# Second attention of a two-layer transformer block: two buffers of turned long tiles, and the value products moved to other steps

## The reference

```python
kf = jnp.repeat(kf, g, axis=1)          # 8 key heads, 4 query heads on each, 64 wide
v = jnp.repeat(v, g, axis=1)
scores = jnp.einsum('bhqd,bhkd->bhqk', q, kf) / jnp.sqrt(jnp.asarray(HD, dt))
scores = jnp.where(causal, scores, jnp.finfo(dt).min)
attn = jax.nn.softmax(scores, axis=-1)
out = jnp.einsum('bhqk,bhkd->bhqd', attn, v)
```

## Time and profile before

| | |
|---|---|
| median of three runs | 2429.59 us |
| the profiled execution | 2425.01 us, of which 2422.9 us are the span |
| TensorE busy | 2127.0 us (88%) |
| VectorE busy | 1499.6 us (62%) |
| ScalarE busy | 891.2 us (37%) |
| GpSimd busy | 511.2 us (21%) |
| mean granted TensorE clock | 0.96 |

### The profile page before, as it was taken

One profiled execution on the slowest core, in us unless ns is written; L12 is line 12 of the kernel. 1 busy time (PEld: TensorE's weight loads), 2 busy tenths in 40 slices (PEclk: granted clock), 3 DMA queues, 4 the chain that ended last, 5 costly groups with the idle time before them and its releaser, 6 DMA issues. The chain is left out here.

```text
span 2422.9 us, 53839 instructions
## 1 busy us (share of the span) xinstructions
PE 2127.0 (88%) x22256; PEld 1484.4 (61%) x22256; DVE 1499.6 (62%) x2380; ACT 891.2 (37%) x1858; POOL 511.2 (21%) x419
## 2 busy tenths in 40 slices
PE   4899969999996999868888988888986788799997
PEld 3677747777775788724444444444444666687776
DVE  4544323333324455468999889988894786177776
ACT  3322123222222300035656556565563232134443
POOL 0110112122220145401111111111112455221111
PEclk9999989999998999979999999999998898899999
DMA  4121144000005633233443334333342866541100
GB/s 153 71 88 36 71 154 144 17 26 17 9 0 212 198 126 122 106 83 83 104 109 90 98 81 112 102 89 98 81 119 85 262 210 194 178 144 52 53 1 35
DMA packets 183984, 242.99 MB, mean 100 GB/s; under 512 B 37744, under 2 KB 110768, under 8 KB 181072
## 3 DMA queue, kind: packets, MB, share of 16 engines
q1 hardware_dynamic: 182896, 239.59, 32.1%
q10 hardware_dynamic: 864, 0.21, 0.0%
HBM read 156.82 MB, written 82.90 MB: 99 GB/s over the span
## 5 line engine op out<-in xcount | busy, mean ns | idle before, releaser
L1479 ACT ACTIVATE a_prob<-ps,a_nmax 128x256 f32<-128x256 f32 (+7 forms) x512 | 377.4, 739 | 349.1 <-DVE a_nmax L1507 212.2
L1592 PE MATMUL ps<-a_kt,a_q 64*128 64x512 f32 (+5 forms) x1536 | 378.0, 533 | 88.0 <-ACT a_prob L1479 64.7
L1507 DVE TENSOR_REDUCE a_nmax<-ps 128x1 f32<-128x1024 f32 (+3 forms) x256 | 256.3, 1001 | 74.1 <-PE ps L1592 72.7
L1524 DVE STREAM_TRANSPOSE a_pt_long<-a_prob 128x512 f32<-128x512 f32 (+3 forms) x512 | 278.3, 582 | 0.0
L1592 PEld LDWEIGHTS ps<-a_kt,a_q 64*128 64x128 f32 x1536 | 142.0, 191 | 186.4 <-ACT a_prob L1479 117.1
L1606 PE MATMUL ps<-a_pt_long,a_v 32*64 32x256 f32 (+3 forms) x7808 | 228.0, 344 | 1.8 <-DVE a_pt_long L1524 0.2
L1991 DVE SCALAR_TENSOR_TENSOR f_part<-ps,f_gu_scale,f_part 128x512 f32<-128x512 f32 x264 | 184.7, 745 | 65.0 <-PE ps L2039 51.7
L1606 PEld LDWEIGHTS ps<-a_pt_long,a_v 32*64 32x64 f32 x7808 | 153.6, 131 | 103.4 <-issue 75.6
L1559 POOL TENSOR_TENSOR a_o<-a_left 128x256 f32<-128x256 f32 x128 | 90.4, 729 | 594.9 <-ACT a_left L1489 594.9
L2039 PE MATMUL ps<-f_xt_hi,f_gu 128*128 128x512 f32 x352 | 142.3, 404 | 22.1 <-DMA f_wd_lo<-scratch_wd 12.6
L843 POOL TENSOR_TENSOR f_hT_lo<-f_h,f_hT_hi 128x512 fp32r<-128x512 f32 x64 | 82.0, 1293 | 325.0 <-ACT f_hT_hi L826 325.0
(11 more groups left out here) (225 smaller groups left out, 4518.5 us busy)
## 6 DMA issues: line engine op xcount, KB each, us to landing
a_q<-scratch_QT SPq DMA_DIRECT2D x512, 64.0 KB, 2.1
scratch_QT<-k_qo SPq DMA_DIRECT2D x64, 256.0 KB, 2.3
a_v<-scratch_V SPq DMA_DIRECT2D x64, 256.0 KB, 4.7
scratch_OT<-a_o SPq DMA_DIRECT2D x32, 512.0 KB, 3.3
o_of<-scratch_OT SPq DMA_DIRECT2D x32, 512.0 KB, 5.5
o_packed<-in_packed SPq DMA_DIRECT2D x11, 768.0 KB, 6.8
f_xt_hi<-scratch_xt SPq DMA_DIRECT2D x8, 1024.0 KB, 7.3
f_xt_lo<-scratch_xt SPq DMA_DIRECT2D x8, 1024.0 KB, 9.1
```

Of the source, the lines that this page charges most:

```text
L1479: last = nc.scalar.activation(prob[:, n % PRING, s].rearrange("p (a w) -> p a w", w=w), SC[n % 2][:, a, 0:w], ACT.Exp, bias=nmax[:, n % 4, ...
L1507: nc.vector.tensor_reduce(nmax[:, n % 4, 0:1], SC[n % 2][:, :, 0:width(0, t)], AX.XY, ALU.max, negate=True).then_inc(maxed, 1)
L1524: last = nc.vector.transpose(pt[hf][:, lo:hi, h, t - FIRST[hf], :], src.rearrange("p (j k) -> p j k", k=32))
L1592: last = pe.matmul(sc[:, a, 0:w], q[r, slot, heads[a * hf], :], kt[r, b, keys], start=not masked, stop=True, skip_group_check=True)
```

## The change

- The long turned tiles get two buffers, used by units in turn: `pt_long` for key blocks 0 to 23 and `pt_wide` for blocks 24 to 31, which only tiles 6 and 7 have.
- Every tile is turned whole, two steps after its scores. A long tile of over 24 blocks takes two instructions (768 columns, and 256 or 128), one of at most 24 blocks takes one (768 or 640 columns). FRONT, BACK and `half_valued` go.
- The short values are placed at r = 26 to 30 (steps 2 to 6 of the next unit) and come ahead of the long ones, which are placed at r = 33 to 46 (steps 9 to 22 of the next unit). The evictions, spreads, scalings and stores follow.
- `rden` gets two buffers. To make room, the ring of queries goes from 4 to 3 and the ring of probabilities from 8 to 4.

```diff
-QRING = 4
-PRING = 8
+QRING = 3
+PRING = 4
...
-LONG_VALUES = {18 + i: range(3 * i, 3 * i + 3) for i in range(10)}
-LONG_VALUES[28] = range(30, 32)
-SHORT_VALUES = {31 + i: range(2 * i, 2 * i + 2) for i in range(8)}
-LONG_LEFT = {28: (0, 1), 29: (2, 3)}
-SHORT_LEFT = {38: (0, 1), 39: (2, 3)}
-LONG_STORE, SHORT_STORE = 34, 44
-LATEST = 45
+MAIN = 24
+LATER = 2
+
+SHORT_VALUES = {26: range(0, 3), 27: range(3, 6), 28: range(6, 9), 29: range(9, 13), 30: range(13, 16)}
+LONG_VALUES = {33: range(0, 2), 34: range(2, 4), 35: range(4, 6), 36: range(6, 8), 37: range(8, 10),
+               38: range(10, 11), 39: range(11, 12), 40: range(12, 14), 41: range(14, 16), 42: range(16, 19),
+               43: range(19, 22), 44: range(22, 25), 45: range(25, 29), 46: range(29, 32)}
+SHORT_LEFT = {31: (0, 1), 32: (2, 3)}
+LONG_LEFT = {47: (0, 1), 48: (2, 3)}
+SHORT_SPREAD, LONG_SPREAD = 27, 40
+SHORT_SCALE, LONG_SCALE = 32, 48
+SHORT_STORE, LONG_STORE = 36, 52
+LATEST = 53
...
-        pt = [sb(f"pt_{s}", [P, BLOCKS[i], HQ, 4, 32]) for i, s in enumerate(("long", "short"))]
+        pt_long = sb("pt_long", [P, 2, MAIN, HQ, 4, 32])
+        pt_wide = sb("pt_wide", [P, 2, BLOCKS[0] - MAIN, HQ, 2, 32])
+        pt_short = sb("pt_short", [P, BLOCKS[1], HQ, 4, 32])
...
-        rden = sb("rden", [P, 16])
+        rden = sb("rden", [P, 2, 16])
...
-                    wait(sp, valued, 2 * u - 1)
+                    wait(sp, valued, 2 * u - 2)
...
-                        act.wait_ge(turned, last_turn(n - PRING))
+                        act.wait_ge(turned, n - PRING + 1)
...
-                def turn(n, part):
+                def turn(n):
                     unit, hf, t, heads = place(n)
-                    if n % USTEPS == 0 and part == FRONT:
-                        wait(dve, half_valued, unit)
-                    elif n % USTEPS in (0, LONG):
-                        wait(dve, valued, 2 * unit + hf - 1)
+                    if n % USTEPS == 0:
+                        wait(dve, valued, order(unit - 2, 0) + 1)
+                    elif n % USTEPS == LONG:
+                        wait(dve, valued, order(unit - 1, 1) + 1)
                     dve.wait_ge(exped, n + 1)
                     blocks = 4 * (t + 1)
...
+                        if hf:
+                            last = nc.vector.transpose(pt_short[:, 0:blocks, h, t, :], src)
+                        else:
+                            near = min(blocks, MAIN)
+                            last = nc.vector.transpose(pt_long[:, unit % 2, 0:near, h, t - 4, :], src[:, 0:near, :])
+                            if blocks > MAIN:
+                                last = nc.vector.transpose(pt_wide[:, unit % 2, 0:blocks - MAIN, h, t - 6, :],
+                                                           src[:, MAIN:blocks, :])
...
                 for n in range(NSTEPS + LATEST):
                     if n < NSTEPS:
                         maxima(n)
-                    for u, r in at_step(n, TURNS):
-                        for i, part in TURNS[r]:
-                            turn(u * USTEPS + i, part)
+                    if LATER <= n < NSTEPS + LATER:
+                        turn(n - LATER)
...
+                    for u, r in at_step(n, SHORT_VALUES):
+                        values(u, 1, SHORT_VALUES[r])
                     for u, r in at_step(n, LONG_VALUES):
                         values(u, 0, LONG_VALUES[r])
-                    for u, r in at_step(n, SHORT_VALUES):
-                        values(u, 1, SHORT_VALUES[r])
```

More of the change, by code:

```diff
@@ L1388, in attention1, with order, turned_part @@
         evicted, o_done, o_stored = sem("evicted"), sem("o_done"), sem("o_stored")
-        half_valued = sem("half_valued")
         def width(hf, t):
             return (t + 1) * P // 2 if hf == 0 else (t + 1) * P
-        turn_order = []
-        for n in range(NSTEPS + LATEST):
-            for u, r in at_step(n, TURNS):
[L1397 to L1401, removed]
+        def order(u, hf):
+            return 2 * u + (1 if hf == 0 else 0)
+        def turned_part(u, hf, j):
+            if hf:
+                return pt_short[:, j], 0
+            if j < MAIN:
+                return pt_long[:, u % 2, j], 4
+            return pt_wide[:, u % 2, j - MAIN], 6
         with nc.Block() as block:
@@ L1461, in _ @@
                     for u, r in at_step(n, (LONG_STORE, SHORT_STORE)):
[L1462 removed]
+                        store_o(u, int(r == SHORT_STORE))
                 sp.wait_ge(o_stored, 16 * 2 * NU)
@@ L1484, in evict @@
                 def evict(u, hf, banks):
-                    half = 2 * u + hf
-                    act.wait_ge(valued, half + 1)
-                    wait(act, o_done, 4 * half)
+                    act.wait_ge(valued, order(u, hf) + 1)
+                    wait(act, o_done, 4 * order(u, hf))
                     for i in banks:
@@ L1519, in turn @@
                     dve.wait_ge(exped, n + 1)
                     blocks = 4 * (t + 1)
-                    lo, hi = {FRONT: (0, MIDDLE), BACK: (MIDDLE, blocks), WHOLE: (0, blocks)}[part]
                     for i, h in enumerate(heads):
-                        src = prob[:, n % PRING, (i * blocks + lo) * 32:(i * blocks + hi) * 32]
-                        last = nc.vector.transpose(pt[hf][:, lo:hi, h, t - FIRST[hf], :],
-                                                   src.rearrange("p (j k) -> p j k", k=32))
+                        src = prob[:, n % PRING, i * blocks * 32:(i + 1) * blocks * 32]
@@ new lines, in turn @@
+                        src = src.rearrange("p (j k) -> p j k", k=32)
+                        if hf:
+                            last = nc.vector.transpose(pt_short[:, 0:blocks, h, t, :], src)
[5 more added lines that the diff above has]
+                                                           src[:, MAIN:blocks, :])
@@ L1526, in turn @@
                     last.then_inc(turned, 1)
                 def invert(u, hf):
-                    half = 2 * u + hf
                     dve.wait_ge(exped, u * USTEPS + (LONG, USTEPS)[hf])
-                    wait(dve, spread_out, half)
-                    nc.vector.reciprocal(rden[:], den[:, hf, :]).then_inc(inverted, 1)
+                    wait(dve, spread_out, order(u - 1, hf) + 1)
+                    nc.vector.reciprocal(rden[:, hf, :], den[:, hf, :]).then_inc(inverted, 1)
                 for n in range(NSTEPS + LATEST):
@@ L1536, in _ @@
                         maxima(n)
-                    for u, r in at_step(n, TURNS):
-                        for i, part in TURNS[r]:
-                            turn(u * USTEPS + i, part)
+                    if LATER <= n < NSTEPS + LATER:
+                        turn(n - LATER)
                     for u, r in at_step(n, (LONG + 2, USTEPS + 2)):
-                        invert(u, r == USTEPS + 2)
+                        invert(u, int(r == USTEPS + 2))
             @block.gpsimd
@@ L1545, in spread_half @@
                 def spread_half(u, hf):
-                    half = 2 * u + hf
-                    pool.wait_ge(inverted, half + 1)
-                    wait(pool, valued, half)
+                    pool.wait_ge(inverted, 2 * u + hf + 1)
+                    wait(pool, valued, order(u, hf))
                     nc.gpsimd.tensor_tensor(spread[:].rearrange("p h t q -> p (h t) q"),
-                                            rden[:].unsqueeze(2).broadcast_to([P, 16, 32]),
+                                            rden[:, hf, :].unsqueeze(2).broadcast_to([P, 16, 32]),
                                             diag[:].unsqueeze(1).broadcast_to([P, 16, 32]), ALU.mult
@@ L1554, in scale_half @@
                 def scale_half(u, hf):
-                    half = 2 * u + hf
-                    wait(pool, o_stored, 16 * half)
+                    wait(pool, o_stored, 16 * order(u, hf))
                     for i in range(4):
-                        pool.wait_ge(evicted, 4 * half + i + 1)
+                        pool.wait_ge(evicted, 4 * order(u, hf) + i + 1)
                         nc.gpsimd.tensor_tensor(o[:, :, :, i, :], left[:, i, 0], left[:, i, 1], ALU.mult
@@ L1563, in _ @@
                 for n in range(NSTEPS + LATEST):
[L1564 to L1567, removed]
+                    for u, r in at_step(n, (SHORT_SPREAD, LONG_SPREAD)):
+                        spread_half(u, int(r == SHORT_SPREAD))
+                    for u, r in at_step(n, (SHORT_SCALE, LONG_SCALE)):
+                        scale_half(u, int(r == SHORT_SCALE))
             @block.tensor
@@ L1598, in value_block @@
                     t0, b, k = FIRST[hf], unit % NB1, j // 4
+                    part, p0 = turned_part(unit, hf, j)
                     for c in range(2):
@@ L1606, in value_block, with denominators @@
                             last = pe.matmul(out[:, :, a - t0:4, :], v[rows, b, j, :],
-                                             pt[hf][rows, j, c::2, a - t0:4, :],
```

(9 more changed lines are left out.)

2 lines of the change are left out of this document (1 added, 1 removed).

## The result

The changed kernel takes 2416.53 us (median of five runs, 2413.06 to 2421.49) against 2430.55 us before (five runs). The ratio is 0.9945, with a 95% interval of 0.993 to 0.996: faster by 14 us (0.6%), where 55 were forecast. The profiled execution took 2421.49 us with a span of 2419.1. It is the slowest of the five, and its mean granted clock (0.950) is the lowest (0.953 to 0.956 in the others), so its trace may show more half-rate pieces than a usual execution has.

A forecast was written before the change was run, and what follows sets the result against it. TensorE and VectorE were taken to bound the kernel in turns within a 49.93 us unit. Sixteen units at 4.1 less (-66) plus 10.6 at the end gave -55: 2370 from the profiled execution, 2375 against the median, range 2362 to 2397.

The forecast's parts named there:

- The wait at step 9: First long value block of a unit: step forecast at 1.92 us, with no wait for the short half's evictions counted.
- Waits that are added or shortened: Term for ring, eviction, GpSimd and SyncE waits: all at zero; late transfer or eviction as rival, chance 0.09, 2383 us.
- step 2: TensorE's first short block waits for step 0's eviction pair, ready at 1.15 against TensorE's 1.28 us: counted as zero.
- The falls of the clock: Rival: TensorE's clock dips at the unit's seam, one dip per unit adding 10 to 23 us (2385 to 2398); chance 0.08.
- The sums by step: Largest of VectorE's work, TensorE's work and the loop per step: 46.6 us a unit, 45.2 in groups; 45.8 taken.
- the loop: Scores, maxima, exponential, then scores two steps on: 1.88 us a step at the long half's tile 7, 1.34 at tile 4.
- The turns: VectorE's long-half turns go from 32 to 24 instructions: 0.6 us less a unit; a 768-column turn takes 0.87.
- The end: Values left after the last scores: TensorE done 25.6 us after the last maxima began, 10.6 more than the 15.0 before.
- The first unit: Steps 18 to 23 lose their long values (13.2 to 9.4 us); 4.4 less in all, counted as 4.1 like other units.
- Query ring: Ring of 3: transfers need 4.0 to 8.0 us against 7.5 available; taken as hidden, bound 0 to 0.5 a unit.
- prob ring: Ring of 4 probabilities: ScalarE waits for a turn that is already done on VectorE, so it costs nothing.
- SyncE: Value loads wait for less; key loads and stores stand behind query-load waits ending four steps ahead of use: zero.

The follow-up runs named there:

- e1: Changed kernel with the short half's two pairs of evictions one step earlier on ScalarE (behind the exponentials of steps 6 and 7): 2382.05 us, ratio 0.9805.
- e5: e1 plus spare score matmuls, one in step 7 and two in step 8: 2382.99 us, ratio 0.982.
- e6: e1 with short values packed into steps 2 to 5, their evictions at steps 5 and 6, long values from step 8 on: 2375.19 us, ratio 0.9785.
- e3: Changed kernel plus spare score matmuls, one in step 7 and two in step 8, evictions unmoved: 2428.68 us, ratio 0.9998.
- e2: Changed kernel with the long half's first value blocks at step 10 instead of 9, evictions unmoved: 2399.64 us, ratio 0.9882.
- e4: Changed kernel's buffers, whole turns and short rings, but value blocks, evictions, spreads, scalings and stores at the earlier kernel's steps: 2415.09 us, ratio 0.9944.

## Why the prediction was wrong

- **The wait at step 9 is the step that failed.** Under "Waits that are added or shortened" the prediction listed the evictions' new steps (7, 8, 23, 0), asked who waits for them at step 2, where TensorE passes with 0.13 to spare, and put the whole term at zero. It did not ask the same at step 9, where the first long block needs the banks of the short half. What was needed stood in its terms. The second pair begins when the exponential of step 8 ends. TensorE, which at that point is ahead by the two score buffers, could score step 9 as soon as the exponential of step 7 had ended. So the block waits for one exponential more than it was given. It cost 1.85 us a unit (47.73 against 45.88), 28 us in the 15 units that have it; e1 gave them back.
- **The falls of the clock** stood among the rivals with 0.08, at 10 to 23 us, at the unit's seam and in steps 7 and 8. They came at steps 8 and 9, and with one piece at the seam of units 0 and 1, for 18.7 us in the profiled execution (2.7 of that kind before). They were not a thing apart: e1 cut them from eight to three units and e5 and e6 to none. The mean clocks of all executions, over the whole kernel, mostly go the same way: their median is 0.954 in the changed kernel, 0.956 in e1, 0.957 in e6 and 0.958 in e5. In e3 and e2 it is lower (0.9515 and 0.952); e2 has fewer falls than the changed kernel, but longer ones (four of its five last 6.8 us, against three of the changed kernel's eight).
- **The books.** From first to last maxima 66 us were forecast to go and 18.1 went in the profiled execution, so 48 are missing. The wait is 28 of them and the falls 16 (18.7 - 2.7). The first unit is 1.5 (below). Another 1.4 is in the count of 16 units: the last maxima open step 23 of the last unit, and that step itself, 2.60 before and 1.19 after, lies outside. The rest is the 0.08 by which a unit without a wait exceeds 45.8. In the medians 41 of the forecast 55 are missing, against some 52 between the profiled executions, so a usual execution has lost less than this account.
- **The sums by step held.** With the wait and the falls out, the unit was 45.88 (45.8 forecast), and the other placements came out at 46.62 (46.6 expected), 49.01 (49.3) and 45.77 (45.4). Taking the largest of the two engines' work and the loop in each step, with neighbours allowed to share, was good to 0.4 us in these four. That 45.8 itself is a choice between the sums 45.2 and 46.6, so its closeness is in part luck.
- **The turns held.** A turn of 768 columns takes 1702.87 - 1701.98 = 0.89 to the next start (0.87 forecast) and one of 128 behind it 1703.06 - 1702.87 = 0.19 (0.20). The timeline of the changed kernel:

```profile
1701.98 0.96 DVE L1527 STREAM_TRANSPOSE a_pt_long<-a_prob 128x768 f32<-128x768 f32 x1
...
1702.87 0.27 DVE L1529 STREAM_TRANSPOSE a_pt_wide<-a_prob 128x128 f32<-128x128 f32 x1
...
1703.06 0.92 DVE L1506 TENSOR_REDUCE a_nmax<-ps 128x1 f32<-128x768 f32 x1
```

- **The end** was mis-sized by 1.3 (26.9 against 25.6). The short values and denominators took 1837.97 - 1831.27 = 6.7 (6.0 forecast) and the long ones 1854.8 - 1840.2 = 14.6 (13.9). Each of these two stretches holds one half-rate piece; what the pieces cost was not tried.
- **The first unit** gave 2.6 (50.78 to 48.14) and not the 4.1 that the sum counts (4.4 by its own terms). Its scores start at the half clock in both kernels, and the changed one shows more half-rate pieces there. How much of it is the clock was not tried.
- **Query ring, prob ring, step 2, SyncE:** from 1095 to 1825 us TensorE waits only for exponentials and, once a unit, at step 9, and e4 with both short rings was faster than before. Taking these as nothing was right for TensorE's waits; no run changed a ring by itself.

So with its evictions one step earlier this placement takes 2382.05 (e1), inside the range that was forecast. The forecast's own 2375 was met by e6 (2375.19), which places the values otherwise; that the two agree to a fraction of a us is chance.

## What to carry to other kernels

When consumers are moved nearer to producers, list for every block that reuses a buffer the instruction that frees it, what stands ahead of that one on its own engine, and by how much the waiting engine may run ahead; do it for each reuse, and not only for the tightest-looking one. An engine that waits in order hands its wait to everything queued behind it, here the next scores. And a wait of TensorE can cost more than its length, since the clock can fall with it: here 28 us of waits went together with 12 us of other losses when one line moved the evictions.

## What the runs showed of the hardware that was not expected

Filling TensorE's idle time ahead of a wait did not keep the clock up. TensorE's idle times in its steps 7 to 9, in an undisturbed unit, and the falls at step 8 or 9 in units 1 to 14:

| kernel | idle times, us | units with a fall |
|---|---|---|
| changed | 0.67, 0.97, 1.93 | 8 |
| e3 | 0.17, 2.01 | 8 |
| e2 | 0.67, 0.96, 0.86 | 5 |
| e1 | 0.67, 0.97 | 3 |
| e6 | 1.48 | 0 |
| e5 | 0.17 | 0 |

Neither the longest idle time nor their sum puts the six in this order (e6 with 1.48 has none and e1 with 0.97 has three; e2 sums to more than e3 and has fewer). Each count is from one profiled execution, so what exactly brings the clock down stays open. The Trainium skill ("TensorE: Matmul & The Clock Gate", "HAM oscillation — how this bites in real kernels") gives, as an abstract rule, only single gaps of idle time that are longer than any in this table. By that rule alone none of these falls should have come, and here they came in up to eight of 14 units.
